# FFN weights stored transposed, and their maxima spread by two TensorE transposes instead of a GpSimd all-reduce

## The chip, the cores and the metric

One core of one Trainium2 chip. The metric is the device time of one execution in microseconds (us); the median of several runs is given. TensorE (PE in the profile), VectorE (DVE), ScalarE (ACT), GpSimd (POOL) and SyncE (SP, which here only issues DMAs) each run their own queue of instructions in order and wait for each other through semaphores.

## What is computed

One transformer layer over 16 batches of 128 tokens of width 256: a cross-attention with 32 heads of 8, and an FFN of width 1024 whose weights and activations are quantised to four bits. Cut to the part that matters here:

```
x = x + attention(layernorm(x), ctx, rope positions, Wq, Wkv, Wout, bout)
xn  = layernorm(x)
x_q = clip(round(xn / s1), -8, 7) * s1
sw1 = max(abs(W1)) / 7;  W1_q = clip(round(W1 / sw1), -8, 7) * sw1      # W1 is 1024 x 256
h   = x_q @ W1_q.T + b1_q                                               # contracted over 256
h_q = clip(round(relu(h) / s2), 0, 15) * s2
sw2 = max(abs(W2)) / 7;  W2_q = clip(round(W2 / sw2), -8, 7) * sw2      # W2 is 256 x 1024
out = x + h_q @ W2_q.T + b2_q                                           # contracted over 1024
```

The maximum of a weight matrix is one number over all of its elements. TensorE contracts over the partitions, so W1 is wanted with its 256 columns on the partitions and W2 with its 1024 columns there, which is the transpose of how both are stored.

## The kernel before, in words

The 16 batches go through a software pipeline of seven stages (S_NORM, S_PROJ, S_STACK, S_MAX, S_ATT, S_OUT, S_FFN, lines 38 to 40). In step s, stage k works on batch s - k, so the pipeline fills over steps 0 to 6; steps 9 to 15 run in a loop. Each step has eight slots g = 0 to 7, and each engine's `body` writes out by hand what it does in which slot. Nothing is scheduled by a planner: an engine's order is the order of its `body`, and a late semaphore holds everything behind it on that engine.

The setup of the FFN weights lies in the filling steps. Lines 411 and 412 load W1 and W2, 1 MB each. VectorE takes the absolute maximum of each partition (`weight_maxima`, line 720) in slot 3 of step 1 and slot 0 of step 2, one 128x1 column each. GpSimd's `partition_all_reduce` (line 534, step 2) turns the two columns into the maxima over all partitions, in every partition. It stands on GpSimd's queue between the norm of step 2 (line 468) and the rotation of step 2 (`rotate`, line 475). VectorE then forms the levels (`prepare_levels`, line 725, slot 2 of step 2) and quantises (`quantise_weights`, line 731, slots 3 and 4): a 2048-element product rounded to int16 into `w_i`, then a clip to bf16 in place. TensorE transposes the 32 blocks of 128x128 in `transpose_weights` (line 1135), eight blocks in each of four slots (`WEIGHT_SLOTS`, line 49: step 2 slots 6 and 7, step 3 slots 1 and 4), into the two banks ps_exp; VectorE and ScalarE copy every four blocks out to `w1T` and `w2T` (`copy_wT`, line 322), four copies each.

The work around it, which the prediction follows: for batch after batch VectorE multiplies by the rope tables (by_cos, by_sin, lines 796 and 801), GpSimd adds them (rot, line 475), ScalarE rounds the sum into q_rows and k_rows (`split_high`, line 582, slots 6 and 7), GpSimd subtracts the rounded part (`split_low`, line 483), and TensorE transposes these rows in the next step (`transpose_rows`, line 1036). ScalarE copies the results to q_comp (line 595) and k_stack (line 601). In step 2 ScalarE's order is: first k_stack copy, v_comp (line 588), q_rows, second k_stack copy, k_rows. After its two subtractions GpSimd clears the second buffer of q_diag (`clear_diagonal`, line 450, 3.5 us, steps 0 and 2 only), and step 3 then starts there with `place_values` (line 486), the norm and the rotation. VectorE's slot 0 of step 3 is the first maximum over scores (`maxima`, line 804) and `split_xT` (line 775), which the second part of `project_qk` on TensorE waits for.

On the host side, `kernel` (line 1210) passes every input as it is.

## Time and profile before

| | |
|---|---|
| median of 3 runs | 298.29 us (298.26 to 298.51) |
| profiled execution: span from the first to the last instruction | 296.1 us |
| between that span and the median run | 2.2 us |
| TensorE busy, share of the span | 250.3 us, 85% |
| VectorE | 223.3 us, 75% |
| ScalarE | 202.2 us, 68% |
| GpSimd | 128.1 us, 43% |
| mean granted TensorE clock | 0.943 |

The profiled execution is listed by its span; its own total time is not listed apart, so the time of the three unprofiled runs stands beside it. The busy times are sums over the whole span and say little of the filling steps, where the stages come in one by one; for these the instructions of a stretch in order of time are read, with the granted clock of that stretch (1.00 is 2.4 GHz, 0.50 is 1.2 GHz).

### The profile page before, as it was taken

How to read it: one execution, taken by the hardware profiler on the slowest of the kernel's cores; microseconds unless marked ns; L12 is line 12 of the kernel's file. 1: busy time of each engine (PE TensorE's matmuls, PEld its weight loads, DVE VectorE, ACT ScalarE, POOL GpSimd, SP SyncE). 2: the span in 40 equal slices, each digit the busy share in tenths (PEclk: the TensorE clock that was granted, in tenths of full speed). 3: DMA queues.
4: the chain of work that ended last, by engine and by line, in shares of the span. 5: the costliest groups of instructions: out<-in, count | busy, mean ns of one | idle time of the engine just before them, and what ended most of it. 6: DMA issues, size and time to landing. Idle time of an engine off the chain costs nothing.

```text
span 296.1 us, 8723 instructions
## 1 busy us (share of the span) xinstructions
PE 250.3 (85%) x2816; PEld 183.8 (62%) x2816; DVE 223.3 (75%) x570; ACT 202.2 (68%) x444; POOL 128.1 (43%) x266
## 2 busy tenths in 40 slices
PE   0056227899999999999999999999999999999653
PEld 0045126867767777777777777777777767665441
DVE  2977418797887979797979797979888877784441
ACT  3213025667679787878787878888887978679423
POOL 7625039444471717263635454445453451520110
PEclk9999557799999999999999999999999999999875
DMA  7921101252111113121211121112112111200101
GB/s 165 340 92 45 35 0 38 62 167 49 37 48 45 45 45 83 41 52 41 80 45 45 40 80 43 45 51 68 44 38 72 41 38 41 72 3 4 35 0 38
DMA packets 31786, 17.41 MB, mean 59 GB/s; under 512 B 6544, under 2 KB 31376, under 8 KB 31760
## 3 DMA queue, kind: packets, MB, share of 16 engines
q1 hardware_dynamic: 29696, 17.06, 21.8%
q10 hardware_dynamic: 2064, 0.02, 0.4%
q8 instruction: 15, 0.25, 0.3%
q14 instruction: 11, 0.09, 0.1%
HBM read 6.31 MB, written 2.10 MB: 28 GB/s over the span
## 4 chain that ended last, share of the span: by engine, by line
PE 69%; issue 11%; DVE 10%; POOL 5%; ACT 4%; DMA 1%; ACTq 0%; POOLq 0%; DVEq 0%
PE ps_misc L972 34%; PE ps_av L972 13%; PE ps_max L972 12%; PE ps_exp L972 9%; DVE turns L697 2%; ACT h_i L636 2%; DVE xn L867 1%; DMA q_diag<-mxT 1%; POOL rot L475 1%; DVE by_cos L796 1%; POOL q_rows L441 1%; DVE by_sin L801 1%; DVE xn L772 1%; POOL k_rows L442 1%; POOL rstd L515 1%
## 5 line engine op out<-in xcount | busy, mean ns | idle before, releaser
L810 DVE TENSOR_REDUCE mx<-ps_max 128x4 f32<-128x512 f32 x128 | 87.3, 686 | 30.0 <-PE ps_max L972 26.9
L607 ACT ACTIVATE expo<-ps_exp 128x512 f32<-128x512 f32 x128 | 77.7, 607 | 19.6 <-PE ps_exp L972 18.1
L972 PE MATMUL ps_exp<-q_diag,k_stack 128*128 128x512 f32 x128 | 60.3, 471 | 0.4 <-DMA q_diag<-mxT 0.4
L972 PE MATMUL ps_av<-expo,v_strip 128*32 128x128 f32 x1024 | 54.1, 285 | 0.0
L972 PE MATMUL ps_max<-k_stack,q_diag 96*128 96x128 bf16 (+1 forms) x512 | 52.9, 226 | 0.8 <-DVE mx L810 0.8
L636 ACT ACTIVATE h_i<-ps_misc,b1q,relu_scale 128x128 int16<-128x128 f32 x128 | 48.3, 470 | 2.5 <-PE ps_misc L972 2.5
L972 PEld LDWEIGHTS ps_max<-k_stack,q_diag 96*128 96x128 bf16 (+1 forms) x512 | 30.8, 99 | 24.5 <-issue 23.3
L500 POOL TENSOR_TENSOR v_strip<-v_comp,zeros 128x32 f32<-128x32 f32 x128 | 28.0, 256 | 19.4 <-PE ps_av L972 19.4
L972 PEld LDWEIGHTS ps_av<-expo,v_strip 128*32 128x32 f32 x1024 | 20.3, 108 | 21.8 <-issue 14.7
L483 POOL TENSOR_TENSOR q_rows<-rot,q_rows 128x256 f32<-128x256 f32 x16 | 11.6, 725 | 36.0 <-ACT q_rows L582 36.0
L972 PEld LDWEIGHTS ps_exp<-q_diag,k_stack 128*128 128x128 f32 x128 | 24.4, 190 | 1.5 <-issue 0.8
L468 POOL TENSOR_TENSOR rstd<-var,minus_half 128x1 f32<-128x1 f32 x16 | 8.9, 557 | 37.4 <-DVE var L766 37.4
L601 ACT CAST k_stack<-ps_misc 128x512 fp32r<-128x512 f32 x32 | 18.9, 590 | 8.6 <-PE ps_exp L972 5.3
L475 POOL TENSOR_TENSOR rot<-by_cos,by_sin 128x512 f32<-128x512 f32 x16 | 20.5, 1282 | 9.5 <-issue 6.9
L972 PE MATMUL ps_misc<-ident,q_rows 128*128 128x128 f32 x128 | 21.1, 291 | 1.8 <-POOL q_rows L483 1.8
L515 POOL TENSOR_TENSOR rstd<-var,minus_half 128x1 f32<-128x1 f32 x16 | 8.8, 549 | 30.8 <-DVE var L860 30.8
L595 ACT CAST q_comp<-ps_misc 128x512 fp32r<-128x512 f32 x32 | 19.1, 596 | 3.8 <-PE ps_misc L972 3.7
L972 PE MATMUL ps_misc<-xqT,w1T 128*128 128x128 bf16 x256 | 20.9, 229 | 0.7 <-ACT xqT L625 0.7
L972 PE MATMUL ps_misc<-ident,k_rows 128*128 128x128 f32 x128 | 19.9, 279 | 1.4 <-ACT v_comp L588 0.7
L972 PE MATMUL ps_misc<-w2T,hq 128*128 128x256 bf16 x128 | 17.7, 282 | 2.0 <-DVE hq L882 1.5
L483 POOL TENSOR_TENSOR k_rows<-rot,k_rows 128x256 f32<-128x256 f32 x16 | 11.7, 734 | 17.4 <-ACT k_rows L582 17.4
L582 ACT CAST q_rows<-rot 128x512 fp32r<-128x512 f32 x16 | 9.8, 613 | 13.1 <-POOL rot L475 13.1
(122 smaller groups left out, 514.3 us busy)
## 6 DMA issues: line engine op xcount, KB each, us to landing
q_diag<-q_comp SPq DMA_DIRECT2D x128, 64.0 KB, 2.0
w<-in_L_ffn_W_dram SPq DMA_DIRECT2D x2, 1024.0 KB, 8.2
out_dram<-y SPq DMA_DIRECT2D x8, 256.0 KB, 2.2
c_in<-in_ctx_dram SPq DMA_DIRECT2D x16, 64.0 KB, 2.1
x_all<-in_x_dram SPq DMA_DIRECT2D x1, 1024.0 KB, 5.8
x_all<-in_x_dram SPq DMA_DIRECT2D x1, 512.0 KB, 4.7
q_diag<-mxT SPq DMA_DIRECT2D x32, 8.0 KB, 1.8
x_all<-in_x_dram SPq DMA_DIRECT2D x2, 128.0 KB, 2.6
```

The source lines that it names most:

```text
L468: pool.tensor_tensor(rstd1[:, r, :], var1[:, r, :], minus_half[:, :], ALU.pow).then_inc(rstd1_ready, 1)
L475: pool.tensor_tensor(rot[:, r, :], by_cos[:, :], by_sin[:, :], ALU.add).then_inc(rot_ready, 1)
L483: pool.tensor_tensor(rows[:, r, :, at:at + HD], src, rows[:, r, :, 0:HD], ALU.subtract)\
L500: ins = pool.tensor_tensor(strips[:, s, :, 9 * s:9 * s + HD], vals, nothing, ALU.add)
L515: pool.tensor_tensor(rstd2[:, r, :], var2[:, r, :], minus_half[:, :], ALU.pow).then_inc(rstd2_ready, 1)
L582: act.copy(rows[:, :, 0:2, :] if n == 0 else rows[:, :, 0:3:2, :], src).then_inc(hi_ready, 1)
L595: act.copy(q_comp[:, r, 4 * half:4 * half + 4, :], src).then_inc(q_ready, 1)
L601: act.copy(k_stack[:, r, 4 * half:4 * half + 4, :], ps_misc[PIECE_BANK[(SK0, SK1)[half]]][:, :].rearrange("p (g t) -> p g t", g=4)).then_i ...
L607: act.activation(expo[:, g % EXPO, :], ps_exp[g % 2][:, :], ACT.Exp, scale=SCALE).then_inc(exp_done, 1)
L636: ins = act.activation(h_i[:, r, f, :], ps_misc[PIECE_BANK[(H0, H1)[half]]][:, 128 * c:128 * c + 128], ACT.Relu, bias=b1q[:, f:f + 1], sca ...
L810: dve.tensor_reduce(out=mx[:, r, 4 * g:4 * g + 4], in_=ps_max[g % 2][:, :].rearrange("p (h k) -> p h k", h=4), axis=AX.X, op=ALU.max).then ...
L972: return pe.matmul(out, lhsT, rhs, start=start, stop=stop, skip_group_check=True, **kw)
```

## The change

Both FFN weights are given to the kernel transposed (W1 as 256 x 1024, W2 as 1024 x 256), so they arrive in the layout of the product operands. The 32 TensorE transposes of weight blocks and the eight copies of their results go. The clip to bf16 writes straight into `w1T` and `w2T`. The all-reduce on GpSimd goes too: TensorE transposes the 128x2 column of partition maxima to 2x128 in ps_exp0, VectorE reduces that to 2x1 and copies it broadcast to 2x128 (`wmax_row`, in the memory of `w_i[0]`), TensorE transposes it to 128x2 in ps_exp1, and VectorE copies it to `wmax_all`. The quantisation of each weight moves back by one slot on VectorE.

```diff
-WEIGHT_SLOTS = [2 * GROUPS + 6, 2 * GROUPS + 7, 3 * GROUPS + 1, 3 * GROUPS + 4]
...
-        w_q = [w_i[0][:, :].bitcast(BF16), w_i[1][:, :].bitcast(BF16)]
...
+        w_q = [w1T[:, :, :, :].rearrange("p c f t -> p (c f t)"), w2T[:, :, :].rearrange("p f d -> p (f d)")]
+        wmax_top = sb("wmax_top", [2, 1])
+        wmax_row = w_i[0][0:2, 0:256].bitcast(F32)
...
-        def copy_wT(eng, n):
...
-            sp.dma_start(w1[:, :, :], w1_d.rearrange("(c p) d -> p c d", p=128)).then_inc(w_loaded, 16)
-            sp.dma_start(w2[:, :, :], w2_d.rearrange("(c p) f -> p c f", p=128)).then_inc(w_loaded, 16)
+            sp.dma_start(w1[:, :, :], w1_d.rearrange("(c p) f -> p c f", p=128)).then_inc(w_loaded, 16)
+            sp.dma_start(w2[:, :, :], w2_d.rearrange("(c p) d -> p c d", p=128)).then_inc(w_loaded, 16)
...
-                if not st.looped and st.s == 2:
-                    pool.wait_ge(wmax_ready, 2)
-                    pool.partition_all_reduce(wmax_all[:, :], wmax[:, :], 128, bass.bass_isa.ReduceOp.max)\
-                        .then_inc(wmax_shared, 1)
...
-                    before = st.s * GROUPS + g - 1
-                    if not st.looped and before in WEIGHT_SLOTS:
-                        copy_wT(act, 2 * WEIGHT_SLOTS.index(before) + 1)
...
+            def spread_maxima():
+
+                steps[0] = 0
+                dve.wait_ge(wmax_in_psum, 1)
+                link(dve.tensor_reduce(out=wmax_top[:, :], in_=ps_exp[0][0:2, 0:128], axis=AX.X, op=ALU.max), wprep)
+                dve.tensor_copy(wmax_row, wmax_top[:, 0:1].broadcast_to([2, 128])).then_inc(wmax_row_ready, 1)
+
             def prepare_levels():
-                steps[0] = 0
-                dve.wait_ge(wmax_shared, 1)
+                dve.wait_ge(wmax_in_psum, 2)
+                dve.tensor_copy(wmax_all[:, :], ps_exp[1][:, 0:2]).then_inc(wmax_copied, 1)
+                dve.wait_ge(wmax_copied, 1)
...
-                dve.tensor_scalar(w_q[n][:, :], w_i[n][:, :], QMIN, QMAX, ALU.max, ALU.min).then_inc(wq_ready, 1)
+                dve.tensor_scalar(w_q[n], w_i[n][:, :], QMIN, QMAX, ALU.max, ALU.min).then_inc(wq_ready, 1)
...
-                elif at == (2, 2):
+                elif at == (2, 1):
+                    spread_maxima()
+                elif at == (2, 3):
                     prepare_levels()
-                elif at in ((2, 3), (2, 4)):
-                    quantise_weights(g - 3)
+                elif at in ((2, 4), (2, 5)):
+                    quantise_weights(g - 4)
...
-                before = st.s * GROUPS + g - 1
-                if before in WEIGHT_SLOTS:
-                    copy_wT(dve, 2 * WEIGHT_SLOTS.index(before))
...
+                if not st.looped and st.s == S_FFN and half == 0:
+                    pe.wait_ge(wq_ready, 2)
...
-            def transpose_weights(n):
...
+            def transpose_weight_maxima():
+
+                pe.wait_ge(wmax_ready, 2)
+                transpose(ps_exp[0][0:2, 0:128], wmax[:, :], ident[:, :]).then_inc(wmax_in_psum, 1)
+
+            def spread_weight_maxima():
+
+                pe.wait_ge(wmax_row_ready, 1)
+                transpose(ps_exp[1][:, 0:2], wmax_row, ident[0:2, 0:2]).then_inc(wmax_in_psum, 1)
...
-                    if g < 2 and not st.looped and st.s == S_ATT:
-                        pe.wait_ge(wT_ready[g], 4)
+                    if g == 0 and not st.looped and st.s == S_ATT:
+                        pe.wait_ge(wmax_copied, 1)
...
-                    at = st.s * GROUPS + g
-                    if not st.looped and at in WEIGHT_SLOTS:
-                        for n in range(2):
-                            transpose_weights(2 * WEIGHT_SLOTS.index(at) + n)
+                    if not st.looped and st.s == 2 and g == 1:
+                        transpose_weight_maxima()
+                    if not st.looped and st.s == 2 and g == 2:
+                        spread_weight_maxima()
...
-        a = _np.ascontiguousarray(inputs[name])
+        a = _np.asarray(inputs[name])
+        a = _np.ascontiguousarray(a.T if name in ('L0_ffn_W1', 'L0_ffn_W2') else a)
```

## Rows read from the trace of the kernel before

**Rows 1.** The page: busy times of the engines; the loads of the FFN weights.
```profile
PE 250.3 (85%) x2816; PEld 183.8 (62%) x2816; DVE 223.3 (75%) x570; ACT 202.2 (68%) x444; POOL 128.1 (43%) x266
...
w<-in_L_ffn_W_dram SPq DMA_DIRECT2D x2, 1024.0 KB, 8.2
```

**Rows 2.** Stretches: PE busy, its weight loads, DVE, ACT, POOL, then granted clock.
```profile
31.50:33.00 1.50, 0.00 (x0) 0.00 (x0) 0.00 (x0) 0.00 (x0) 0.20 (x1) 0.50 0.17 43
43.00:46.00 3.00, 2.92 (x20) 2.74 (x20) 1.42 (x3) 1.31 (x3) 2.47 (x2) 0.50 0.00 0
...
65.00:280.00 215.00, 210.77 (x2545) 152.63 (x2544) 176.11 (x467) 173.64 (x389) 93.61 (x207) 1.00 0.19 48
```

**Rows 3.** GpSimd in order of time, steps 2 and 3: start, duration (us), instruction.
```profile
32.80 0.37 POOL L534 PARTITION_ALL_REDUCE wmax_all<-wmax  x1 [5.63 <-issue]
40.06 1.25 POOL L475 TENSOR_TENSOR rot<-by_cos,by_sin 128x512 f32<-128x512 f32 x1 [6.89 <-issue]
...
43.53 0.73 POOL L483 TENSOR_TENSOR k_rows<-rot,k_rows 128x256 f32<-128x256 f32 x1 [0.77 <-ACT k_rows L582]
44.20 3.52 POOL L452 MEMSET q_diag<- 128x4096 int32 x1
47.67 1.73 POOL L500 TENSOR_TENSOR v_strip<-v_comp,zeros 128x32 f32<-128x32 f32 x8
49.35 0.61 POOL L468 TENSOR_TENSOR rstd<-var,minus_half 128x1 f32<-128x1 f32 x1
49.92 1.28 POOL L475 TENSOR_TENSOR rot<-by_cos,by_sin 128x512 f32<-128x512 f32 x1
```

**Rows 4.** The instructions of line 534.
```profile
L534 POOLq MODIFY_POOL_CONFIG  x2: 11/11/11, 27.1 to 27.2; - x2
```

**Rows 5.** VectorE in order of time, steps 2 and 3.
```profile
23.98 2.27 DVE L722 TENSOR_REDUCE wmax<-w 128x1 f32<-128x2048 f32 x1
...
27.40 0.41 DVE L801 TENSOR_TENSOR by_sin<-ps_misc,sin_pos 128x256 f32<-128x256 f32 x1
...
33.60 1.28 DVE L733 TENSOR_SCALAR w_i<-w,w_levels 128x2048 int16<-128x2048 f32 x1
34.92 0.69 DVE L734 TENSOR_SCALAR w_i<-w_i 128x2048 bf16<-128x2048 int16 x1
...
44.12 0.69 DVE L810 TENSOR_REDUCE mx<-ps_max 128x4 f32<-128x512 f32 x1 [6.25 <-PE ps_max L972]
45.27 0.56 DVE L779 TENSOR_TENSOR xT_lo<-ps_misc,xT_hi 128x384 fp32r<-128x384 f32 x1 [0.46 <-ACT xT_hi L571]
...
48.97 0.41 DVE L801 TENSOR_TENSOR by_sin<-ps_misc,sin_pos 128x256 f32<-128x256 f32 x1
...
49.99 1.36 DVE L772 TENSOR_SCALAR xn<-x_all,mv,rstd 128x256 f32<-128x256 f32 x1
...
52.81 0.27 DVE L818 CAST mxT<-ps_misc 16x128 fp32r<-16x128 f32 x1
...
54.12 0.41 DVE L330 COPY w2T<-ps_exp 128x512 bf16<-128x512 bf16 x1
```

**Rows 6.** TensorE in order of time.
```profile
27.73 0.66 PE L972 MATMUL ps_misc<-ident,k_rows 128*128 128x128 f32 x4 [0.68 <-ACT q_comp L595]
...
30.15 0.76 PE L972 MATMUL ps_misc<-ident,k_rows 128*128 128x128 f32 x4 [0.46 <-ACT v_comp L588]
...
43.08 0.59 PE L972 MATMUL ps_exp<-ident_bf,w_i 128*128 128x128 bf16 x4 [4.47 <-ACT w1T L330]
...
63.37 0.50 PE L972 MATMUL ps_exp<-q_diag,k_stack 128*128 128x512 f32 x1 [0.40 <-DMA q_diag<-mxT]
```

**Rows 7.** VectorE near the clearing of q_diag in step 0.
```profile
7.88 4.65 DVE L697 TENSOR_SCALAR turns<-ang 128x64 int32<-128x64 f32 x1
```

**Rows 8.** GpSimd near the clearing of q_diag in step 0.
```profile
7.77 1.25 POOL L448 TENSOR_TENSOR wkv_lo<-wkv,wkv_hi 128x512 fp32r<-128x512 f32 x1
8.97 3.50 POOL L452 MEMSET q_diag<- 128x4096 int32 x1
```

More of the change, by code:

```diff
@@ L164, in xattn_ffn_kernel @@
         b1q = sb("b1q", [128, FC])
[L165 to L166 removed]
+        w1 = sb("w1", [128, DC, FFN])
+        w2 = sb("w2", [128, FC, DIM])
         w_i = [sb("w1_i", [128, 2048], I16), sb("w2_i", [128, 2048], I16)]
[L168 removed]
         w1T = sb("w1T", [128, DC, FC, 128], BF16)
         w2T = sb("w2T", [128, FC, DIM], BF16)
+        w_q = [w1T[:, :, :, :].rearrange("p c f t -> p (c f t)"), w2T[:, :, :].rearrange("p f d -> p (f d)")]
+        wmax_top = sb("wmax_top", [2, 1])
+        wmax_row = w_i[0][0:2, 0:256].bitcast(F32)
         s_act = sb("s_act", [128, 2])
@@ L259, in xattn_ffn_kernel @@
         wmax_ready = sem("wmax_ready")
-        wmax_shared = sem("wmax_shared")
+        wmax_in_psum = sem("wmax_in_psum")
+        wmax_row_ready = sem("wmax_row_ready")
         wq_ready = sem("wq_ready")
-        wT_in_psum = sem("wT_in_psum")
-        wT_ready = sems("wT_ready")
+        wmax_copied = sem("wmax_copied")
         pads_ready = sem("pads_ready")
@@ L320, in xattn_ffn_kernel @@
         block = stack.enter_context(nc.Block())
-        def copy_wT(eng, n):
-            src = ps_exp[n % 2][:, 0:256].bitcast(BF16).rearrange("p (f c) -> p f c", f=4)
-            which, c, quarter = n // 4, n // 2 % 2, n % 2
-            fs = slice(4 * quarter, 4 * quarter + 4)
-            dst = w1T[:, c, fs, :] if which == 0 else w2T[:, fs, 128 * c:128 * c + 128]
-            eng.wait_ge(wT_in_psum, n + 1)
-            copy = eng.tensor_copy if eng is nc.vector else eng.copy
-            copy(dst, src).then_inc(wT_ready[n % 2], 1)
-        w_flat = [w1[:, :, :].rearrange("p c d -> p (c d)"), w2[:, :, :].rearrange("p c f -> p (c f)")]
+        w_flat = [w1[:, :, :].rearrange("p c f -> p (c f)"), w2[:, :, :].rearrange("p f d -> p (f d)")]
         out_pairs = out_d.rearrange("(k two) t d -> k t two d", two=2)
@@ L1133, in project_y @@
                 ins.then_inc(y_in_psum, 1)
-            def transpose_weights(n):
-                which, c, quarter = n // 4, n // 2 % 2, n % 2
-                pe.wait_ge(wq_ready, which + 1)
-                if n >= 2:
-                    pe.wait_ge(wT_ready[n % 2], n // 2)
-                ps = ps_exp[n % 2][:, 0:256].bitcast(BF16)
-                for f in range(4):
-                    fc = 4 * quarter + f
-                    at = fc * DIM + 128 * c if which == 0 else c * FFN + 128 * fc
-                    ins = transpose(ps[:, 128 * f:128 * f + 128], w_q[which][:, at:at + 128], ident_bf[:, :])
-                ins.then_inc(wT_in_psum, 1)
+            def transpose_weight_maxima():
[4 more added lines that the diff above has]
+                transpose(ps_exp[1][:, 0:2], wmax_row, ident[0:2, 0:2]).then_inc(wmax_in_psum, 1)
             def body(st):
```

2 lines of the change are left out of this document (removed).

## The prediction

> **What bounds the kernel now.** I read the page first. TensorE is busy for 250.3 us of 296.1 [rows 1], and the stretches show where the rest is: from 65 to 280 us it is busy for 210.8 of 215 us at the full granted clock [rows 2]. That stretch is bound by TensorE, and the change touches nothing in it. Whatever the change brings must come from the filling steps, and must reach the start of that stretch, the score product for the exponentials at 63.37 us, which waited for a DMA of the maxima and after which TensorE hardly pauses [rows 6].
>
> So the filling was read next, engine by engine in order of time. GpSimd was free 5.63 us before its all-reduce at 32.80, that is at 27.17, and the rotation behind it starts 6.89 us after the all-reduce ends, at 40.06 [rows 3]. Both gaps have "issue" as their releaser: nothing that the profile shows was waited for. The rope terms that the rotation adds were complete at 27.81 [rows 5]. The two configuration instructions for the pool at 27.1 to 27.2 [rows 4] say what the first gap is: code is exchanged for the all-reduce. The reader is to see that one instruction with 0.37 us of span holds GpSimd for 12.9 us, from 27.17 to 40.06, and with it the rotation of step 2 and everything that follows from it: the subtraction that ends at 44.26, the clearing of q_diag, the placing of values, and the rotation of step 3 at 49.92, with hardly a pause between the last four [rows 3]. TensorE is empty in part of it at the 1.2 GHz level of its clock [rows 2].
>
> The profiled execution has a span of 296.1 us; the median run took 298.29, so 2.2 us lie around the span, and I leave them as they are. Gains below are taken off the span and so off 298.29. About 0.2% of it, 0.6 us, is what a measurement of this kernel can tell from no change.
>
> **The change, part by part.** I follow the time at which each engine reaches a landmark, old against new; the difference is the gain so far.
>
> Rotation of step 2. The all-reduce is gone, so it starts just after 27.81: 27.9 for 40.06, a gain of 12.2 us, and it ends at 29.15.
>
> The two small transposes. The first waits for the second column of maxima, complete at 26.25 [rows 5], and stands before the second query transposes: they and the copy behind them come up to 0.5 us later, my estimate for the little that it is behind project_qk. VectorE's reduction of 2x128 out of PSUM is priced by the nearest row, the 16x128 cast at 0.27 us [rows 5]: done at 28.05. The broadcast copy costs at least 0.15 us, as one more small operation. TensorE's second transpose waits for it, and behind that wait stand the key transposes that ran at 27.73 [rows 6]. If the copy runs at once they start at 28.5, a delay of 0.8 us. If it is held while the rotation has GpSimd's port they start at 29.4, a delay of 1.7. No row shows a broadcast copy beside a GpSimd instruction, so both ends stay; the nearest one, xn beside a rotation, took 1.36 us and ended 0.15 after the rotation [rows 3, 5], so I take the upper half, 1.5.
>
> By the Trainium skill ("VectorE: DVE Perf Modes", section "Mode 2×_2P") a one-source operation between SBUF operands with an even outermost dimension takes both ports, fp32 too, which would put this copy at the upper end and the sum 0.2 us later than mine; no run shown here can say.
>
> From there ScalarE and TensorE alternate in the order of the code: first k_stack copy, v projection, v_comp, second key transposes. These ended at 30.91 [rows 6], now at 32.4. Second k_stack copy, k_rows rounding and GpSimd's second subtraction follow, some 0.6, 0.6 and 0.73 us: 34.4 for the old 44.26, a gain of 9.9. Note that 2.3 of the 12.2 us are lost here, because ScalarE and TensorE had finished that part during the stall and now have not.
>
> The quantisation. It ran at 33.60 to 37.5 while GpSimd stood still [rows 3, 5]: 1.28 and 0.69 us per weight, 3.9 in all. The levels now need one more small copy out of PSUM, 0.2 us, and the quantisation starts near 30.2, so it falls onto the two subtractions and the clearing. What happens then is shown in step 0: a 128x64 scalar operation that VectorE began at 7.88, during a GpSimd subtraction, lasted 4.65 us, past the end of that subtraction and until the 3.50 us clearing that came directly behind it was over [rows 7, 8]. I take the same here. The subtractions wait for at most the rest of one VectorE operation, I put 0.3 us: the clearing then runs from 34.6 to 38.1, against 44.20 to 47.72, a gain of 9.6. The last clip, which would be done at 34.1 without this, waits for the clearing and ends near 38.5.
>
> By the Trainium skill ("SBUF — State Buffer", section "SBUF: two separate sides") the shared pair is locked for a whole instruction by whichever starts first. Read strictly, the waiting clip would get it between subtraction and clearing, and the sum would be that of the first rival below; the row of step 0 speaks for the other outcome.
>
> VectorE in step 3. Its first maximum moves from 44.12 to 38.4. From that to the second by_sin, at 49.38, were 5.3 us [rows 5], in part at TensorE's pace. Now the scores and the first passes of the projection are already done when VectorE comes: maximum and xT_lo (1.1 us), TensorE's five remaining passes (1.1, estimated from 0.21 us apart at half clock), the rope terms (1.35). That is 42.0, a gain of 7.4. The rotation then starts at 42.1 for 49.92, and xn ends at 43.5 for 51.35: a gain of 7.8. So what is late next is not GpSimd, which is through with clearing, values and norm (1.7 and 0.6 us) at about 41.6, but VectorE.
>
> The removed transposes and copies. Eight copies go, four on VectorE at 0.41 us [rows 5], one like it on the way from xn to step 4's start at each of two places; I count 0.65 us on the path. On TensorE 32 blocks go, one group of four of which took 0.59 [rows 6]; eight of them stood between the transposed maxima and the next scores, 0.55 us on the path. ScalarE's four copies lie beside these. Together 1.2 us. Their cover elsewhere was the stall itself.
>
> Costed at nothing: the loads. They stay two transfers of 1 MB, 8.2 us to landing [rows 1], and only swap which has the short rows; VectorE's first reduction of them runs long after. The wait for wq_ready in step 6 comes long after the quantisation. SyncE issues q_diag's DMAs after the clearing and the query copies, both of which move with the landmarks above; its order is unchanged. The late loads for ScalarE's rounding of Wout are issued ahead of all steps. If one of these were late, up to the gain at that point would be lost.
>
> **Sum.** 7.8 + 1.2 = 9.0 us at the start of step 4, carried unchanged to 63.37 (now 54.4) and from there to the end: 298.29 - 9.0 = **289.3 us**.
>
> **The rivals.** First, the clip slips in before the clearing, or the quantisation never meets the subtractions. Then GpSimd leads: clearing ends at 38.1 to 38.7, values and norm follow, the rotation of step 3 comes near 40.9, a gain of 9.0 plus 1.2: 288.1. For it speaks that GpSimd waits for ScalarE before each subtraction, so that there are pauses in which VectorE can get in. Without any cost from the port and with the copy at once, landmarks are 1 us earlier again, 287.0.
>
> Second, the change doesn't remove all of the stall. The configuration before the all-reduce accounts for the gap of 5.63 us; the 6.89 us behind it have no instruction of their own [rows 3]. If they belong to something else on GpSimd's queue, the rotation starts at 34.8, the quantisation is over without collision, and about 6.1 us are gained: 292.2. Against it: no other place on this queue shows such a gap. By the Trainium skill ("GPSIMD Engine Reference", section "Instruction dispatch") the first call of a freshly loaded kernel pays about 6 us, which by itself covers one gap and says nothing of the other.
>
> Third, the clock. TensorE was at 1.2 GHz from 31.5 and through a dense stretch, in which 20 matmuls took 2.92 us, 0.146 each, against 0.083 in the long stretch [rows 2]. A full step has 174 matmuls by the code, 14.4 us; at the lower level it would take 11 us more. Before, the density after the stall raised the clock before TensorE became the bound. If the thinner work now leaves it low into step 4 or 5 for half a full step, 5.5 us go back: 294.8. The decisive point is 0.8 of a full step, where the 9.0 us are used up; beyond, at one and a half steps, the kernel is slower than before, 305.7. For it speaks that the removed transposes are TensorE work in the filling; against it, that steps 4 and 5 are themselves dense.
>
> **How the numbers follow.** Forecast 289.3: 0.46. Port mostly harmless, 287.0 to 288.1: 0.36. Second gap stays: 0.05. Clock low for half a step or so: 0.07. Clock low beyond the decisive point, slower: 0.04. Gain eaten to within 0.2%: 0.02. The range reaches down to the harmless port less a little for the small terms, 286.7, and up by 2 us over the forecast for the sizes of the collisions and a short piece of low clock, 291.3. Faster 0.94, same 0.02, slower 0.04.
>
> **What would show it.** In the profile of the changed kernel: rotation of step 2 at about 27.9, with no "issue" gap on GpSimd; xn of step 2 stretched to about 1 us by it; key transposes at 28.5 to 29.4; a clip or product of the quantisation lasting 3 us or more over the clearing; the clearing near 34.6; VectorE's first maximum near 38.4; rotation of step 3 near 42.1; TensorE dense from 54.4. A first maximum at 34 with a rotation at 41 would be the first rival, a gap at 28 the second, a clock of 0.50 after 56 the third. A long stretch that isn't the same length as before would make all of it wrong.

## The result, and the profile after

The changed kernel takes 289.35 us (median of 4 runs, 288.7 to 289.54) beside 298.4 (4 runs, 298.26 to 300.06): a ratio of 0.969 with a 95% interval of 0.9656 to 0.9723, 9.05 us less. The forecast was 289.3. The number came out; part of the way to it did not, and that part is what this section and the experiments are about. The medians are over all runs, while the ratios leave out a run more than 1.5% above the fastest of its kernel, which is one of the ten with the all-reduce put back and one of the six with the second clearing on ScalarE.

The page of the changed kernel, busy times of the engines, as [rows 1]:

```profile
PE 249.2 (87%) x2786; PEld 181.8 (63%) x2786; DVE 223.0 (78%) x569; ACT 200.0 (70%) x440; POOL 128.2 (45%) x265
```

TensorE has 30 instructions less (32 block transposes gone, two small ones come), everything else is nearly as before. The profiled execution, the fastest of the four, took 288.7 us with a span of 286.9, so 1.8 us lie around the span. GpSimd in order of time in steps 2 and 3 (start, duration, instruction), to be held beside [rows 3]:

```profile
27.72 1.27 POOL L465 TENSOR_TENSOR rot<-by_cos,by_sin 128x512 f32<-128x512 f32 x1 [0.73 <-DVE by_sin L792]
32.45 1.32 POOL L473 TENSOR_TENSOR q_rows<-rot,q_rows 128x256 f32<-128x256 f32 x1 [3.46 <-ACT q_rows L568]
34.24 0.73 POOL L473 TENSOR_TENSOR k_rows<-rot,k_rows 128x256 f32<-128x256 f32 x1 [0.47 <-ACT k_rows L568]
34.91 3.52 POOL L442 MEMSET q_diag<- 128x4096 int32 x1
...
40.57 1.26 POOL L465 TENSOR_TENSOR rot<-by_cos,by_sin 128x512 f32<-128x512 f32 x1
```

The rotation of step 2 starts at 27.72 for 40.06; there is no gap with "issue" left in these steps. The configuration instructions for the pool are gone with the all-reduce. The rotation of step 3 follows at 40.57 for 49.92, so of 12.3 us, 9.35 are left one step on. VectorE in the same stretch, beside [rows 5]:

```profile
27.56 0.27 DVE L712 TENSOR_REDUCE wmax_top<-ps_exp 2x1 f32<-2x128 f32 x1
27.86 1.20 DVE L713 COPY w_i<-wmax_top 2x128 f32<-2x128 f32 x1
...
29.98 1.29 DVE L724 TENSOR_SCALAR w_i<-w,w_levels 128x2048 int16<-128x2048 f32 x1
...
31.91 1.28 DVE L724 TENSOR_SCALAR w_i<-w,w_levels 128x2048 int16<-128x2048 f32 x1
33.22 1.10 DVE L725 TENSOR_SCALAR w2T<-w_i 128x2048 bf16<-128x2048 int16 x1
34.24 0.68 DVE L801 TENSOR_REDUCE mx<-ps_max 128x4 f32<-128x512 f32 x1
...
40.64 1.34 DVE L763 TENSOR_SCALAR xn<-x_all,mv,rstd 128x256 f32<-128x256 f32 x1 [1.89 <-POOL rstd L458]
```

Here the reader sees VectorE and GpSimd hold each other up at the port that they share, three times. The durations and their ends say so: each stretched instruction ends at most 0.6 us after the other engine's did. The broadcast copy of 2x128 elements took 1.20 us, until the rotation of 27.72 had ended. GpSimd's first subtraction, 0.73 us elsewhere, took 1.32 from 32.45, because the product of 31.91 was under way. The second clip, 0.69 elsewhere, took 1.10 from 33.22, because that subtraction was. But it had ended at 34.32, before the clearing began at 34.91, and VectorE's first maximum came at 34.24, not 38.4. After that VectorE waits for GpSimd: 1.89 us before xn at 40.64.

TensorE in order of time, beside [rows 6]:

```profile
29.12 0.22 PE L962 MATMUL ps_exp<-ident,w_i 2*128 2x2 f32 x1 [1.75 <-DVE w_i L713]
29.27 0.65 PE L962 MATMUL ps_misc<-ident,k_rows 128*128 128x128 f32 x4
...
31.91 1.12 PE L962 MATMUL ps_misc<-ident,k_rows 128*128 128x128 f32 x4 [0.46 <-ACT v_comp L574]
...
42.73 0.37 PE L962 MATMUL ps_misc<-ident,mx 128*16 128x128 f32 x1 [2.92 <-DVE mx L801]
...
53.45 0.50 PE L962 MATMUL ps_exp<-q_diag,k_stack 128*128 128x512 f32 x1
```

The key transposes wait for the broadcast copy, 29.27 for 27.73. The second ones, at 31.91, took 1.12 us where they took 0.76 before [rows 6]: from 31 to 34 us the granted clock was 0.50 here, while before it was 1.00 until 30 and 0.78 from there to 31. Between 39.8 and 42.73 TensorE has nothing to do, and the stretches show what its clock did (PE busy, weight loads, DVE, ACT, POOL, granted clock, DMA share, GB/s):

```profile
40.00:42.00 2.00, 0.00 (x0) 0.00 (x0) 1.36 (x2) 0.43 (x1) 1.83 (x3) 0.77 0.37 75
42.00:44.00 2.00, 1.27 (x8) 1.22 (x8) 1.85 (x4) 0.00 (x0) 0.00 (x0) 0.50 0.17 36
...
46.00:48.00 2.00, 2.00 (x14) 1.82 (x13) 1.39 (x3) 1.59 (x4) 0.93 (x3) 0.53 0.48 102
48.00:50.00 2.00, 2.00 (x22) 1.91 (x20) 1.83 (x7) 1.99 (x3) 2.00 (x6) 1.00 0.67 154
62.00:240.00 178.00, 177.40 (x2144) 130.55 (x2137) 150.70 (x399) 146.40 (x328) 84.50 (x188) 1.00 0.22 50
```

It fell during the empty stretch to 0.50, 1.2 GHz, and was back at 1.00 from about 48; by these rows it was low for 6.8 us. The long stretch from 62 on is as dense as before: 177.4 of 178 us at 1.00, the same as from 72 to 250 before.

### The profile page after: what moved, and what is told of

It reads as the page before. It is cut to its first block, busy times and chain, and to the rows that moved or that the text cites. A ratio compares the mean times of both kernels' runs of the same rounds, so it can differ in the third digit from the quotient of the medians.

```text
span 286.9 us, 8646 instructions
## 1 busy us (share of the span) xinstructions
PE 249.2 (87%) x2786; PEld 181.8 (63%) x2786; DVE 223.0 (78%) x569; ACT 200.0 (70%) x440; POOL 128.2 (45%) x265
## 4 chain that ended last, share of the span: by engine, by line
PE 71%; DVE 10%; issue 7%; POOL 6%; ACT 5%; ACTq 0%; POOLq 0%; DVEq 0%
PE ps_misc L962 36%; PE ps_av L962 13%; PE ps_max L962 13%; PE ps_exp L962 9%; DVE red L681 2%; ACT h_i L622 2%; POOL v_strip L490 1%; DVE xn L858 1%; POOL q_rows L473 1%; DVE by_sin L792 1%; DVE by_cos L787 1%; POOL q_diag L442 1%; POOL q_rows L431 1%; DVE xn L763 1%; POOL k_rows L432 1%
## 5 line engine op out<-in xcount | busy, mean ns | idle before, releaser
L490 POOL TENSOR_TENSOR v_strip<-v_comp,zeros 128x32 f32<-128x32 f32 x128 | 27.9, 255 | 19.7 <-PE ps_av L962 19.7
L473 POOL TENSOR_TENSOR q_rows<-rot,q_rows 128x256 f32<-128x256 f32 x16 | 12.2, 764 | 38.6 <-ACT q_rows L568 38.6
L962 PE MATMUL ps_misc<-ident,q_rows 128*128 128x128 f32 x128 | 20.5, 286 | 1.8 <-POOL q_rows L473 1.7
L962 PE MATMUL ps_misc<-w2T,hq 128*128 128x256 bf16 x128 | 18.6, 291 | 2.0 <-DVE hq L873 1.5
L962 PEld LDWEIGHTS ps_misc<-xqT,w1T 128*128 128x128 bf16 x256 | 15.6, 102 | 4.3 <-issue 1.2
```

Source lines behind the costliest of these rows:

```text
L473: pool.tensor_tensor(rows[:, r, :, at:at + HD], src, rows[:, r, :, 0:HD], ALU.subtract)\
L490: ins = pool.tensor_tensor(strips[:, s, :, 9 * s:9 * s + HD], vals, nothing, ALU.add)
L962: return pe.matmul(out, lhsT, rhs, start=start, stop=stop, skip_group_check=True, **kw)
```

## The experiments

Each kernel ran on the chip beside the kernel before (298.3 to 298.7 in the three series). The runs of one kernel scatter by 0.6 to 5 us here, so next to the medians the start of the same instruction is compared in the profiles: the rotation (rot) of GpSimd, once for each of the 16 batches. Each profile is one execution, and the clock falls at different moments in different executions, so small differences between two profiles are read with the clock beside them.

**The two parts of the change, one at a time.** First the all-reduce back, transposed weights kept; `transpose_weight_maxima`, `spread_maxima` and `spread_weight_maxima` go with their calls:

```diff
+                    pool.wait_ge(wmax_ready, 2)
+                    pool.partition_all_reduce(wmax_all[:, :], wmax[:, :], 128, bass.bass_isa.ReduceOp.max)\
+                        .then_inc(wmax_shared, 1)
...
+                elif at == (2, 2):
+                    prepare_levels()
+                elif at in ((2, 3), (2, 4)):
+                    quantise_weights(g - 3)
```

> The changed kernel (289.35 us) with the maxima spread by the GpSimd all-reduce again; the transposed weights stay, so the 32 block transposes and eight copies stay away. Theory (the stall of 12.9 us on GpSimd is the whole matter, the removed transposes are worth at most the 1.2 us of the prediction): both gaps return, the rotation of step 2 is at 40 again, 297.1 to 298.2 us. Rival (the block transposes and their copies, whose waits also fill the time around the stall, carry a good part): 292 to 295 us.

Measured 298.69 us (10 runs, 297.88 to 302.75), ratio 1.0026 (1.0 to 1.0052). GpSimd in this kernel:

```profile
32.70 0.37 POOL L524 PARTITION_ALL_REDUCE wmax_all<-wmax  x1 [5.53 <-issue]
39.73 1.25 POOL L465 TENSOR_TENSOR rot<-by_cos,by_sin 128x512 f32<-128x512 f32 x1 [6.66 <-issue]
...
49.11 1.26 POOL L465 TENSOR_TENSOR rot<-by_cos,by_sin 128x512 f32<-128x512 f32 x1
```

Both gaps are back, 5.53 and 6.66 us. The transposed weights alone bring nothing that can be measured: the median is half a us above the expected interval's end, and the rotation of step 3 is 0.8 us earlier than before, 0.3 of it from the rotation of step 2.

Then the reverse, the kernel before with only the maxima changed; the two small transposes on TensorE and `spread_maxima` on VectorE come in as in the change:

```diff
-                    pool.wait_ge(wmax_ready, 2)
-                    pool.partition_all_reduce(wmax_all[:, :], wmax[:, :], 128, bass.bass_isa.ReduceOp.max)\
-                        .then_inc(wmax_shared, 1)
```

> The kernel before with nothing changed but the maxima, which are spread by the two TensorE transposes; block transposes and copies are back. Theory: nearly the whole gain, 289.7 to 290.6 us, the rest being the copies on VectorE and ScalarE and the eight blocks before the scores. Rival (the two parts need each other, since the block transposes now stand in TensorE's queue behind a quantisation that collides with GpSimd): 291.5 us or more.

Measured 289.48 us (4 runs, 288.74 to 290.39), ratio 0.9702 (0.9667 to 0.9737): all of the gain, 0.13 us from the changed kernel by the medians. The profile says more than the medians can. TensorE, ScalarE and then GpSimd of this kernel in order of time:

```profile
32.60 1.12 PE L982 MATMUL ps_misc<-ident,k_rows 128*128 128x128 f32 x4 [0.46 <-ACT v_comp L588]
33.51 1.06 PE L982 MATMUL ps_exp<-ident_bf,w_i 128*128 128x128 bf16 x8
```

```profile
34.60 0.58 ACT L334 COPY w1T<-ps_exp 128x512 bf16<-128x512 bf16 x1 [0.27 <-PE ps_exp L982]
```

```profile
35.78 0.73 POOL L487 TENSOR_TENSOR k_rows<-rot,k_rows 128x256 f32<-128x256 f32 x1 [1.92 <-ACT k_rows L582]
36.45 3.51 POOL L456 MEMSET q_diag<- 128x4096 int32 x1
...
42.12 1.26 POOL L479 TENSOR_TENSOR rot<-by_cos,by_sin 128x512 f32<-128x512 f32 x1
```

The second subtraction starts 1.5 us later than in the changed kernel (35.78 for 34.24), and the rotation of step 3 at 42.12 for 40.57. Not all of that is the block transposes: 0.69 us was there before the first of them ran, since TensorE's key transposes and v projection were slower in this execution (the second key transposes start at 32.60 for 31.91). The other 0.85 is ScalarE's wait for a group of blocks and its copy. At the last rotations the difference in these two profiles is 1.35 us. So the transposes and copies cost 0.85 us ahead of the rotation of step 3; what they cost behind it is shown under the clock below. The medians of these two kernels show no difference.

**What the second gap is.** A second all-reduce directly behind the first:

```diff
+                    pool.partition_all_reduce(wmax_again[:, :], wmax[:, :], 128, bass.bass_isa.ReduceOp.max)
```

> The kernel before with a second all-reduce of the same columns directly behind the first, into a tile that nobody reads. It tells what the 6.9 us after the all-reduce are. If they are an exchange of code back to the usual one (and the 5.6 us before it the exchange to the all-reduce's), a second call behind the first costs its own span only: 0.4 to 1.5 us more than before, 298.8 to 299.9. If the 6.9 us are the all-reduce itself, whose span in the trace is rough: 6.9 more, about 305. If each call pays both: 12.9 more, about 311.

Measured 298.49 us (10 runs, 298.29 to 300.95), ratio 1.0018 (0.9995 to 1.0042), 0.2 us more than the 298.28 beside it, just under the first of the three forecasts and far from the other two.

```profile
32.80 0.37 POOL L535 PARTITION_ALL_REDUCE wmax_all<-wmax  x1 [5.67 <-issue]
33.09 0.43 POOL L537 PARTITION_ALL_REDUCE wmax_again<-wmax  x1
40.70 1.25 POOL L476 TENSOR_TENSOR rot<-by_cos,by_sin 128x512 f32<-128x512 f32 x1 [7.17 <-issue]
```

The second call took 0.43 us, and the gap behind the pair is 7.17. So the gaps of 5.6 and about 7 us belong to the pair as a whole, one ahead of it and one behind, and not to each call. That fits an exchange of GpSimd's code there and back. The exchange itself leaves no instruction in the trace: the first gap has two configuration instructions ahead of it, the second none, so that the second is an exchange too is inferred. The Trainium skill ("GPSIMD Engine Reference", section "Instruction dispatch") gives approximately 6 us for the first call of a freshly loaded kernel, with no visible instruction. The first gap agrees, with 5.5 to 5.7 us; of the way back, the larger half of the cost here, the page says nothing.

**The copy that the rotation holds.** Moved to ScalarE:

```diff
-                dve.tensor_copy(wmax_row, wmax_top[:, 0:1].broadcast_to([2, 128])).then_inc(wmax_row_ready, 1)
+                        act.wait_ge(wprep, 1)
+                        act.copy(wmax_row, wmax_top[:, 0:1].broadcast_to([2, 128])).then_inc(wmax_row_ready, 1)
```

> The changed kernel with the broadcast copy of 2x128 on ScalarE instead of VectorE. Theory (the copy took 1.20 us because the rotation on GpSimd held the port that both share, and it held the key transposes on TensorE, which lead by way of ScalarE to GpSimd's clearing): the key transposes start at 28.5 instead of 29.27, the clearing and all behind it 0.5 to 0.8 us earlier, 288.6 to 288.9 us. Rival (what is won there is lost in later collisions of the quantisation with GpSimd's subtractions): 289.2 to 289.5.

Measured 289.47 us (4 runs, 287.65 to 291.73), ratio 0.9728 (0.9659 to 0.9796): not told apart from the changed kernel. The mechanism is in the profile: the copy took 0.30 us on ScalarE, and the key transposes started at 28.28 for 29.27. GpSimd in order of time:

```profile
31.63 1.73 POOL L473 TENSOR_TENSOR q_rows<-rot,q_rows 128x256 f32<-128x256 f32 x1 [2.72 <-ACT q_rows L568]
33.42 1.07 POOL L473 TENSOR_TENSOR k_rows<-rot,k_rows 128x256 f32<-128x256 f32 x1
34.44 3.50 POOL L442 MEMSET q_diag<- 128x4096 int32 x1
...
40.11 1.25 POOL L465 TENSOR_TENSOR rot<-by_cos,by_sin 128x512 f32<-128x512 f32 x1
```

But of that 1.0 us only 0.47 reach the clearing. The v projection took 0.17 us longer in this execution, and the second subtraction took 1.07 us for 0.73, since VectorE's last clip was under way; that is another 0.35. The first subtraction was stretched as well (1.73), but the second would not have been ready earlier. So the mechanism of the theory and that of the rival are both there; the medians decide nothing.

**A quantisation during the clearing.** This tests the step of the prediction that did not happen:

```diff
-                elif at in ((2, 4), (2, 5)):
-                    quantise_weights(g - 4)
+                elif at in ((2, 4), (3, 0)):
+                    quantise_weights(st.s - 2)
```

> The changed kernel with the second weight quantised in slot 0 of step 3 instead of slot 5 of step 2, so that its product and clip meet GpSimd's clearing of q_diag (34.9 to 38.4 us). Theory (a product or clip that comes during the clearing waits until its end, as the scalar operation of step 0 did): one of the two lasts over 3 us, VectorE is through near 39.5 instead of 34.3, the rotation of step 3 comes near 42.5 instead of 40.57, and the time is 1.5 to 2.5 us longer, 290.9 to 291.9 us. Rival (the clearing only writes and does not keep VectorE out): VectorE has the 2 us of work in time that it spends waiting, 289.2 to 289.8 us, and neither operation is longer than 1.3 us.

Measured 291.12 us (4 runs, 290.65 to 292.19), ratio 0.9747 (0.9713 to 0.9781), 1.8 us more than the changed kernel. VectorE and then GpSimd in order of time:

```profile
35.61 4.05 DVE L724 TENSOR_SCALAR w_i<-w,w_levels 128x2048 int16<-128x2048 f32 x1
```

```profile
35.07 3.51 POOL L442 MEMSET q_diag<- 128x4096 int32 x1
38.54 3.21 POOL L490 TENSOR_TENSOR v_strip<-v_comp,zeros 128x32 f32<-128x32 f32 x8
...
42.62 1.26 POOL L465 TENSOR_TENSOR rot<-by_cos,by_sin 128x512 f32<-128x512 f32 x1 [0.37 <-DVE by_sin L792]
```

The product that began at 35.61 took 4.05 us, past the end of the clearing at 38.58, and in turn the placing of values took 3.21 us for 1.71. The rotation of step 3 came at 42.62, as expected. So the mechanism exists as predicted and costs some 2 us; in the changed kernel the clip was through 0.6 us before the clearing began.

**The clearing on the path.** In the changed kernel GpSimd leads from the second subtraction through the clearing. It was moved to ScalarE, idle in step 1:

```diff
+                act.copy(q_diag[:, r, :, :].rearrange("p g t -> p (g t)"), zeros[:, 0:1].broadcast_to([128, GROUPS * 512]))\
+                    .then_inc(zeros_ready, 1)
...
-                if not st.looped and st.s in (0, 2):
+                if not st.looped and st.s == 0:
```

> The changed kernel with the second buffer of q_diag cleared on ScalarE in step 1, behind the sine, where it is idle, instead of on GpSimd in step 2. Theory (GpSimd's queue leads from the second subtraction through the 3.5 us clearing and the placing of values to the rotation of step 3, as the chain of waits shows): the placing starts at 35 instead of 38.4, the rotation waits for the rope terms instead and comes near 38.3 instead of 40.57, 286.8 to 287.6 us. Rival (VectorE or TensorE at half clock take over at once, or the clearing on ScalarE delays step 1 as much): 288.6 us or more.

Measured 287.68 us (6 runs, 284.72 to 289.25), ratio 0.9584 (0.9544 to 0.9625). The rotation of step 3 came at 38.65 and that of step 4 at 48.93, 3.0 us ahead of the changed kernel, and then all of it was lost by step 5 in this execution, which took 288.27 us. The chain of waits shows where:

```profile
47.62 4.37 DMA q_diag<-mxT
...
52.03 0.49 PE ps_exp L970
```

The DMA of the maxima was 4.37 us under way behind the 1 MB load of x (issued at 46.02), and TensorE waited 1.59 us for it; its clock fell to 0.50 behind that. In the changed kernel 3.3 us lay between the two issues and the DMA took 2.8 us; here it was 1.6 us, and without a load in front the same DMA takes 1.8 us (median). The median of 287.68 lies just above the theory's range.

**The clock.** 24 operations of the identity with itself in the empty stretch, as products and as transposes:

```diff
+                        pe.wait_ge(wmax_copied, 1)
+                        for _ in range(24):
+                            mm(ps_exp[0][:, 0:128], ident[:, :], ident[:, :])
```

> The changed kernel with 24 products of the identity with itself, 128x128 fp32, on TensorE in slot 4 of step 3, into a bank that is free there; nothing reads them. They fill most of the 2.9 us in which TensorE stood empty from 39.8 to 42.7 while its granted clock fell to 0.50. Theory (the part of the gain that is missing after the rotation of step 3 went to TensorE's work from 42.7 to 47.7 at the lower level): the clock stays at 1.00 there, the start of step 4 and the long stretch come 0.7 to 1.5 us earlier, 287.9 to 288.7 us. Rival (the work there waits for VectorE and ScalarE, and a faster TensorE only waits longer): 289.2 to 289.6 us.

Measured 294.03 us (6 runs, 293.83 to 294.47), ratio 0.984 (0.9816 to 0.9864). The experiment was mis-sized: an fp32 product is two instructions where a transpose is one, so the 48 of them took 5.52 us instead of some 2.9 and became the path themselves. It says nothing of the clock's price.

> As the run with 24 filler products, with the same 24 operations issued as transposes. Theory (what keeps the clock up is that TensorE has instructions, of whatever kind): the same as with products, within 0.3 us, and the clock at 1.00 from 42.7 on. Rival (transposes do not count, as the Trainium skill says in the page TensorE: Matmul & The Clock Gate, section Part 4: PE-mode transpose): the clock falls to 0.50 as without them, and the time is that of the changed kernel, 289.2 to 289.6 us.

Measured 290.51 us (6 runs, 289.53 to 290.9), ratio 0.971 (0.9683 to 0.9736). TensorE of this kernel in order of time, then its stretches (columns as above):

```profile
39.93 2.78 PE L962 MATMUL ps_exp<-ident 128*128 128x128 f32 x24
...
54.28 0.50 PE L962 MATMUL ps_exp<-q_diag,k_stack 128*128 128x512 f32 x1 [1.36 <-DMA q_diag<-mxT]
```

```profile
40.00:42.00 2.00, 2.00 (x20) 2.00 (x19) 0.82 (x1) 0.59 (x1) 2.00 (x6) 1.00 0.33 71
42.00:44.00 2.00, 1.43 (x15) 1.20 (x13) 2.00 (x5) 0.00 (x0) 0.39 (x1) 1.00 0.33 68
```

With nothing but fp32 transposes in the empty stretch the clock stayed at 1.00, and the passes of the v projection behind it took 0.28 us for 0.41 in the changed kernel. The Trainium skill ("TensorE: Matmul & The Clock Gate", section "Part 4: PE-mode transpose") says that transposes do not count as TensorE being busy in the same way; this run shows the contrary for these. The time did not fall, because step 4 reached the same DMA too early: it was issued 2.3 us behind the load of x and took 4.13 us, TensorE waited 1.36 us for it at 54.28, and the clock was at 0.50 from 56 to 58 behind that.

What the clock costs shows in the stretch from the rotation of step 3 to that of step 4, as one row for each of five kernels: the changed one, the kernel before, the one with only the maxima changed, and, from further down, the one with the load of x moved and the same with 20 filler transposes.

```profile
40.57:51.94 11.37, 9.11 (x69) 7.68 (x69) 9.32 (x20) 6.04 (x11) 6.33 (x15) 0.70 0.49 131
```

```profile
49.92:61.47 11.55, 9.66 (x85) 8.24 (x85) 9.92 (x23) 7.57 (x14) 6.34 (x15) 0.85 0.42 115
```

```profile
42.12:53.70 11.58, 9.55 (x85) 7.91 (x83) 9.85 (x22) 7.21 (x13) 6.34 (x14) 0.85 0.46 133
```

```profile
39.84:50.56 10.72, 8.27 (x69) 6.98 (x69) 9.18 (x20) 6.34 (x12) 6.31 (x15) 0.84 0.23 50
```

```profile
41.17:51.47 10.30, 8.73 (x88) 6.82 (x86) 9.66 (x20) 6.46 (x12) 6.35 (x15) 1.00 0.24 52
```

Columns are as above, with the duration of the stretch behind its bounds and the granted clock third from the end. Four kernels with the clock at 1.00 need 10.28 to 10.30 us for it, this one with its 24 transposes among them (the 24 products are the exception). At 0.84 it takes 10.72 to 10.91 us in three kernels. At 0.70 it takes 11.37 in the changed kernel and 11.35 in the one with the all-reduce back. So the clock costs the changed kernel 1.1 us here. With the block transposes it takes 11.55 and 11.58 us at 0.85, and 12.15 at 0.86 in the kernel with two all-reduces: at nearly the same clock the transposes and copies cost some 0.85 us here as well. The changed kernel doesn't show that, since its clock was low for longer. That removing them is what left TensorE empty for longer (2.92 us for 1.80 ahead of the transposed maxima) and so cost part of the clock fits the medians, but no run tests it.

**The load of x moved**, from the start of step 4 to that of step 3, alone and with two of the edits above:

```diff
-                if not st.looped and st.s in (2, 4):
-                    load(3 if st.s == 2 else 4)
+                if not st.looped and st.s in (2, 3):
+                    load(st.s + 1)
```

> The changed kernel with the last load of x (1 MB, batches 8 to 15) issued at the start of step 3 instead of step 4. In the changed kernel it is issued 3.3 us before the DMA of the maxima that step 4 waits for, and its work there hid the transfer: the score product behind that DMA ran at 53.45 with almost no wait. Theory: nothing to be won while step 4 is reached that late, 289.0 to 289.5 us. Rival (the load slows the DMAs of q_diag in step 4 already now): 288.0 us or less.

Measured 287.81 us (5 runs, 287.04 to 288.75), ratio 0.9658 (0.963 to 0.9685). The theory was wrong: 1.5 us less by the medians, though the intervals touch. In its profile 0.9 us of the lead is there before the load is even issued, at the rotation of step 1, and is scatter between executions; the other 0.77 arises by step 5. Most of that, 0.65, arises from the rotation of step 3 to that of step 4, where its clock happened to be low for half as long (the rows above). At the DMA itself, which took 1.8 us for 2.8, 0.25 us is gained. How much of the 1.5 us by the medians is the load stays open; the run with the filler below has the load moved too and nearly the same time.

With the filler as well, as 20 transposes:

```diff
+                        for _ in range(20):
+                            mm(ps_exp[0][:, 0:128], ident[:, :], ident[:, :], is_transpose=True)
```

> The changed kernel with the last load of x issued in step 3 and 20 filler transposes on TensorE in slot 4 of step 3, whose kind was seen to keep the clock at 1.00 (24 of them, 2.8 us). It prices the lower clock of 42.7 to 47.7 us without the DMA stall that hid it in the run with 24. Theory: step 4 starts earlier by 0.7 to 1.5 us than without the filler, 287.9 to 288.7 us. Rival (waits for VectorE and ScalarE take the place of the slower TensorE): within 0.3 us of the run with the early load alone.

Measured 287.48 us (5 runs, 287.1 to 287.82), ratio 0.9639 (0.9613 to 0.9664), within 0.35 us of the run with the load alone. From the rotation of step 3 to that of step 4 this kernel needed 10.30 us with the clock at 1.00, and the one with the load alone 10.72 at 0.84: the filler brings 0.4 us over that execution, where the run with 24 transposes brought 1.1 over the changed kernel's. This profile starts the stretch 1.3 us later than the one with the load alone, 0.8 of it from step 1, so its lead does not show in the total. The theory's mechanism is there, smaller than forecast; by the medians (0.33 us) the rival's range is just missed and the theory's too.

And the second clearing on ScalarE together with the early load:

> The run with the second clearing on ScalarE, and the last load of x issued at the start of step 3. Theory (in that run the rotation of step 4 was 3.0 us earlier than in the changed kernel and all of it was lost in one place, where the DMA of the maxima took 4.37 us behind the 1 MB load of x issued 1.6 us before it, and TensorE stood): without the load in front the DMA takes about 2 us, the stall of 1.6 us and the fall of the clock behind it go, and 2.5 to 3.0 us of the lead last to the end, 286.3 to 286.9 us. Rival (something else in step 4 holds at the same time, ScalarE or VectorE): 287.5 us or more.

Measured 284.18 us (5 runs, 283.7 to 285.7), ratio 0.9535 (0.9503 to 0.9567), 2 us better than the theory. The score product behind the DMA ran at 50.44 without a wait. From the rotation of step 4 to that of step 5 it took 12.53 us, for 15.84 in the run with the clearing alone, so the stall with the low clock behind it had cost 3.3 us, about the 3.5 between the two medians. The lead over the changed kernel at the last rotation is 3.2 us, in an execution of 285.45 us. Why the median is 2 us below the forecast is open in part: the forecast was built on one execution of 288.27 us.

The version that beats both, the kernel before and the changed one, adds to this the first clearing on ScalarE, ahead of the sine, and the copy of the maxima there:

```diff
-                if not st.looped and st.s in (0, 2):
-                    clear_diagonal(st.s // 2)
...
+                        clear_half(0)
                         act.wait_ge(ang_ready, 1)
                         act.activation(trig[:, :, :], red[:, 3, :, :], ACT.Sin).then_inc(trig_ready, 1)
+                        clear_half(1)
```

> The run before it with two more edits: the first clearing of q_diag also on ScalarE, ahead of the sine in step 0, and the broadcast copy of the maxima on ScalarE. Theory: the scalar operation of the rope tables that waited 4.65 us for the clearing in step 0 now waits only for the end of GpSimd's subtraction, so that the tables are ready 3.4 us earlier; the sine comes 2.9 us earlier, behind a clearing of 3.6 us on ScalarE; the copy gives another 0.5 us. Some 2.5 to 3.2 us less than the run without these two edits, 283.2 to 284.3 us. Rival (step 1 then waits for loads or for ScalarE): a gain of 1.5 us or less over that run.

Measured 281.3 us (6 runs, 279.6 to 282.39), ratio 0.9431 (0.9399 to 0.9464), 8 us less than the changed kernel and 2.9 us less than the run before it, within the forecast gain of 2.5 to 3.2; the time in us was forecast 2 us too high because the run before it was. VectorE in step 0 of this kernel, beside [rows 7]:

```profile
6.65 1.17 DVE L689 TENSOR_SCALAR turns<-ang 128x64 int32<-128x64 f32 x1
...
12.09 0.15 DVE L701 COPY red<-red 128x1 f32<-128x1 f32 x1
```

The scalar operation that took 4.65 us takes 1.17. In the changed kernel it was the cast behind it that waited, 4.63 us from 7.96; here that cast takes 1.19. The sine's input is complete at 12.24 for 15.80 in the run before it, and the rotation of step 1 comes at 16.52 for 20.09.

## Why the prediction was right, and where it was not

**What bounds, and the stall: right.** Everything came from the filling. The rotation of step 2 was predicted at 27.9 and came at 27.72. Both gaps left with the all-reduce; the run with the all-reduce back loses the whole gain and the run with only the maxima changed has it. The second rival, that the gap of 6.89 us stays, is refuted.

**The broadcast copy: right, the way from it to the clearing 0.6 us short.** The copy was taken near its upper end, held by the rotation; it was, 1.20 us. The key transposes were put at 29.2 and came at 29.27. The loss by the second subtraction was put at 2.3 of 12.2 us and came at 3.0 (it ends at 34.97 for 44.26, a gain of 9.3 where 9.9 was said). The subtractions' waits for VectorE are not the reason: the first was stretched by 0.6 us, but the second waited for ScalarE after it (0.47 us) and took its usual 0.73. The reason is TensorE's pace: the second key transposes were to end at 32.4 and ended at 33.03, since the v projection took 0.85 us for 0.62 and they themselves 1.12 for 0.76, with the granted clock at 0.50 from 31 to 34. The prediction had carried the old durations over. Some other profiles (the one with only the maxima changed, for instance) show the same slow instructions here with a granted clock of 1.00, so that the clock is the cause is likely, not shown.

The Trainium skill ("VectorE: DVE Perf Modes", section "Mode 2×_2P") says that such a copy takes both ports, and this duration agrees: 1.20 us beside the rotation, 0.30 on ScalarE. No run has the copy on VectorE without a GpSimd instruction beside it. With the copy on ScalarE, VectorE's xn stands in its place and takes 1.27 us where it takes 0.40 behind the rotation.

**The clearing: the step that failed.** "The last clip, which would be done at 34.1 without this, waits for the clearing and ends near 38.5." It ended at 34.32. I had taken the pattern of step 0, where the clearing came directly behind a subtraction while VectorE waited. In step 2 there are two subtractions with 0.47 us between, in which GpSimd waits for ScalarE, and the waiting clip got in behind the first and was through 0.6 us before the clearing. The clearing itself held nothing up, and GpSimd instead of VectorE led to the rotation of step 3. This was the first rival, with 0.36 of the chance together with its variant, and its signs are those the prediction gave: a first maximum at 34, a rotation at 41. The run with the late quantisation shows that the mechanism itself is real and that the outcome hung on 0.6 us. The rule of the Trainium skill ("SBUF — State Buffer", section "SBUF: two separate sides"), that whoever starts first has the port for a whole instruction, is not at odds with either: what decided was who was ready in the gap.

**The sum: right by luck, from errors that cancel.** At the rotation of step 3 the gain is 9.35 us where 7.8 was said, 1.55 too little, because the clearing did not strike. Behind it the 1.2 us for the removed transposes and copies came out at 0.57: the score product at 53.45 for 63.37 is a gain of 9.92 where 9.0 was said. Of that 0.57, 0.18 is there by the rotation of step 4 (11.37 us for 11.55), and 0.39 is the wait for the DMA of the maxima [rows 6], which is not there after. The size of the term was not the error. At nearly equal clock the rows above put it at some 0.85 us from the rotation of step 3 to that of step 4, and the run with the maxima alone at another 0.85 ahead of the rotation of step 3, some 1.7 in all. What the sum left out, at nothing, is the clock in the empty stretch: 1.1 us of those 11.37. The kernel before lost to it in its 11.55 as well, by the rows at 0.84 some 0.4 (an estimate), so some 0.7 is the change's. So the forecast had a cost of the port that did not come, and lacked a clock that did and the loss of the next paragraph; together they came near the measured time by luck.

"Carried unchanged to the end" lost 0.7: the gain is 9.66 at the last rotation, 222.51 for 232.17, and 9.2 at the end of the span, 286.9 for 296.1. The last loss is in the emptying pipeline. Eight products of the last but one batch, y, took 1.06 us before and 1.90 after, in the chains of waits (start, duration, what) of the kernel before and of the changed one:

```profile
283.62 1.06 PE ps_misc L972 x8
```

```profile
273.99 1.90 PE ps_misc L962 x8
```

Before, the granted clock had come back to 1.00 there; after, it stayed at 0.50. This goes with the execution and not with the change: the kernel before with a second all-reduce took 1.90 us there at 0.50, and the changed kernel with the late quantisation 1.06 at 1.00. Why the clock comes back in one execution and not in the other stays open. For the same reason the median's agreement to 0.05 us is chance; the interval of the ratio is some 1 us to either side.

Two numbers of the prediction do not follow from the terms given for them. For the second rival, 5.3 us at the rotation of step 2 and 1.2 for the transposes make 6.5 us, not 6.1. And GpSimd, said to be through with clearing, values and norm at about 41.6, is by its terms (38.1, 1.7 and 0.6) through at 40.4; it was at 40.61.

**The clock as a rival: right to be unlikely, wrong to be left out of the sum.** The third rival wanted half a full step of dense work at the lower level, and its sign, 0.50 after 56, is not there. But the clock did fall, for 6.8 us before that, and cost 1.1 us.

## What to carry to other kernels

A cross-partition reduction on GpSimd can cost far more than its span: look for the gaps with no releaser on both sides of it, and ask whether anything on that queue is wanted within the next 13 us, the time that it was held here. Here two small transposes did the same for 0.6 us of TensorE and 1.6 of VectorE. A large stall also hides things: here it hid a 3.5 us clearing, a port shared by two engines and a 1 MB load in front of a small urgent one, and removing those brought nearly as much again (281.3 us from 289.35) as removing it had. When an operation waits for a shared port, look at the gaps between the other engine's instructions, not only at their sum. And before a size is read off two profiles, compare the granted clock in the same stretch: here a lower clock hid most of what the removed transposes were worth.

## What the runs showed of the hardware that I had not expected

The gap behind the all-reduce is longer (6.7 to 7.2 us) than the one ahead of it (5.5 to 5.7), and two calls in a row pay each once. The port works against both sides: a 128x256 subtraction on GpSimd stretched from 0.73 to 1.73 us behind a product of 1.28, and placing values from 1.71 to 3.21. ScalarE clears the same 128x4096 elements in 3.6 us, as long as GpSimd (3.5), and no wait for it shows: GpSimd's 128x512 subtraction beside it took 1.27 us, as elsewhere. An 8 KB DMA took 1.8 us by itself, 2.8, 4.1 and 4.4 when issued 3.3, 2.3 and 1.6 us behind a 1 MB load. Twenty fp32 transposes held TensorE's granted clock at 1.00 through a stretch where without them it fell to 0.50.
